# Reordering the first attention layer of a two-layer attention and mixture-of-experts kernel on all engines

## The reference, cut to what matters

```python
xn = ln(x, g_norm)
q = (xn @ Wq).reshape(b, n, 16, 64)            # 16 heads of 64
k, v = split(xn @ Wkv)                         # one shared key/value head
k, v = concat([null_k, k]), concat([null_v, v])
q = l2norm(q) * q_scale                        # l2norm: t / max(norm(t), 1e-12)
k = l2norm(k) * k_scale
sim = q @ k^T * 8 + bias                       # masked, causal
out = softmax(sim) @ v
return ln(out @ Wout, g_out)
...
x = x + ternary_ffn(attention_0(x))            # first layer
x = x + mixture_of_experts(attention_1(x))     # second layer: no l2norm of q and k
```

## Time and profile before

| | |
|---|---|
| three timed runs | 679.77, 673.1, 679.88 us; median 679.77 |
| profiled execution | 673.8 us |
| its span, first to last instruction | 672.1 us |
| granted TensorE clock, mean over the span | 0.921 of full speed |
| busy: PE, DVE, ACT, POOL | 73%, 63%, 56%, 48% of the span |
| first layer's scores | from 55.8 us on, 16 batches |
| second layer's scores | from 348.4 us on, 16 batches |

### The profile page before, as it was taken

How to read it: one execution, slowest core, us unless ns; L and a number is a source line. 1 busy time by engine, 2 the same in 40 slices (tenths; PEclk the granted TensorE clock), 3 DMA queues, 4 the chain that set the end, 5 groups by cost and what they waited for, 6 DMA issues and landing times.

```text
span 672.1 us, 13998 instructions
## 1 busy us (share of the span) xinstructions
PE 493.2 (73%) x3209; PEld 397.8 (59%) x3209; DVE 426.6 (63%) x2098; ACT 378.4 (56%) x1473; POOL 322.8 (48%) x397
## 2 busy tenths in 40 slices
PE   1057788888788887888679899999886505999930
PEld 0034566666566655756668787787775403887820
DVE  2644788778877888446367989888997421344313
ACT  1036876777677767465178787878685101444310
POOL 5235476446654683176343434252347660345660
PEclk9986999999999998999679999999999855999975
DMA  3822075220000000000000000000001112344316
GB/s 102 213 61 74 13 133 109 68 64 9 4 6 6 4 6 4 1 1 1 4 5 9 6 8 5 6 6 5 7 18 44 35 44 50 103 116 124 88 38 193
DMA packets 53757, 30.14 MB, mean 45 GB/s; under 512 B 19994, under 2 KB 50131, under 8 KB 53715
## 3 DMA queue, kind: packets, MB, share of 16 engines
q1 hardware_dynamic: 51154, 24.77, 15.7%
q0 software_dynamic: 2560, 4.90, 2.3%
HBM read 16.13 MB, written 11.42 MB: 41 GB/s over the span
## 4 chain that ended last, share of the span: by engine, by line
PE 39%; DVE 18%; issue 14%; SPq 10%; ACT 7%; DMA 6%; POOL 5%; DVEq 1%; POOLq 0%; ACTq 0%
PE psS L810 5%; PE psS L1061 5%; PE psQ L782 4%; DVE sc L1430 4%; DMA slot_rows<-Y,dest_u 4%; PE psQ L777 3%; PE psQ L1051 3%; PE psO L846 3%; ACT sc L1143 2%; SPq L448 2%; ACT qT L1124 2%; PE psA L865 2%; DVE centred L1494 2%; SPq L431 2%; DVE OT L1451 2%
## 5 line engine op out<-in xcount | busy, mean ns | idle before, releaser
L1143 ACT ACTIVATE sc<-sc,negmax 128x97 f32<-128x97 f32 (+3 forms) x512 | 179.2, 355 | 55.3 <-DVE negmax L1430 55.1
L1430 DVE CUSTOM_DVE_ANT_0 sc<-psS,wide_buf 128x97 f32<-128x97 f32 (+3 forms) x512 | 93.7, 239 | 65.2 <-PE psS L810 64.2
L810 PE MATMUL psS<-kk,qT 128*128 128x194 f32 (+3 forms) x512 | 102.7, 323 | 17.9 <-DVE negmax L1430 17.8
L613 POOL TENSOR_TENSOR wide_buf<-bias,mask 128x132 f32<-128x132 f32 (+3 forms) x128 | 104.3, 841 | 6.1 <-DVE negmax L1430 4.2
L810 PEld LDWEIGHTS psS<-kk,qT 128*128 128x128 f32 x512 | 81.1, 194 | 34.6 <-issue 30.7
L1143 ACT ACTIVATION_READ_ACCUMULATOR sc<-sc,negmax 128x1 f32 x512 | 97.8, 191 | 0.0
L1442 DVE TENSOR_TENSOR pn<-sc,rsum 128x128 f32<-128x128 f32 (+3 forms) x128 | 71.5, 559 | 8.7
L865 PE MATMUL psA<-Wo,OT 128*128 128x128 f32 (+1 forms) x512 | 65.5, 282 | 1.7 <-DVE OT L1451 1.7
L865 PEld LDWEIGHTS psA<-Wo,OT 128*128 128x128 f32 x512 | 62.9, 196 | 3.0 <-DVE OT L1451 2.6
L562 POOL TENSOR_TENSOR qrn<-qssc,half 128x9 f32<-128x9 f32 (+1 forms) x32 | 57.3, 1789 | 2.7
L588 POOL TENSOR_SCALAR qssc<-qss 128x9 f32<-128x9 f32 (+1 forms) x32 | 13.0, 405 | 91.8 <-DVE qss L1416 91.8
(11 more groups left out here) (256 smaller groups left out, 1022.2 us busy)
## 6 DMA issues: line engine op xcount, KB each, us to landing
eW<-in_L_ffn_W SPq DMA_DIRECT2D x16, 256.0 KB, 3.0
slot_rows<-empty SPq DMA_DIRECT2D x2, 1390.0 KB, 11.7
xb<-slot_rows SPq DMA_DIRECT2D x16, 139.0 KB
vp_u<-vp SPq DMA_DIRECT2D x128, 8.0 KB
choice_rows<-zero_row SPq DMA_DIRECT2D x8, 256.0 KB, 3.0
wide_buf<-choice_rows SPq DMA_DIRECT2D x8, 256.0 KB, 4.5
Wq<-in_L_cond_Wq SPq DMA_DIRECT2D x2, 512.0 KB, 6.9
vp_u<-vp SPq DMA_DIRECT2D x64, 16.0 KB
```

What stands on the lines that cost most here:

```text
L613: pool.tensor_tensor(unit_masked(i, u).rearrange("p h e k -> p (h e) k"), unit_bias(layer, u).rearrange("p h e k -> p (h e) k"), mask[laye ...
L810: m = pe.matmul(psS[:, h, 0:2 * w], qT[i][:, h, u].rearrange("p m q -> p (m q)"), kk[i][:, :, 0:w], start=True, stop=True)
L1143: m = act.activation(v, v, ACT.Exp, bias=negmax[:, u, g:g + 1], scale=-1.0, accum_out=psum_row[:, u, g:g + 1])
L1430: dve.tensor_tensor_reduce(sc[u][:, h, e, :], unit_psum(u)[:, h, e, :], unit_masked(i, u)[:, h, e, :], -1.0, -FAR, ALU.add, ALU.min, accum ...
```

## The change

Only the order and the waits of the first attention layer change, and one small operation moves from one engine to another. The arithmetic is the same.

1. The floor of the squared sums goes from POOL (`q_norm`) to DVE (`floored`), one for each half, shortly behind the sum. POOL keeps only the power (`q_rsqrt`).
2. `project_in` of the first layer is split: keys and values (`project_values`), first half of the queries, second half (`project_heads`). It projects `b+1` in the pass of `b`, instead of `b+2` at its end: the first half ahead of the scores of unit 0, the second half between units 0 and 1.
3. `turn_queries` is split. The first half of `b+1` stays in the pass of `b`, the second half opens the pass of `b+1`. On DVE `queries_norm` is split likewise.
4. Unit 3 of a batch is pushed back into the next pass on ACT and DVE: its `biased`, exponentials and `divide`, and `divide` of unit 2.
5. `queries` on ACT counts each half on `q_ready`, so a half of the projection waits only for its own half.
6. In the out norm the mean and variance (`moments`) are taken ahead of `keys_in`, and `out_centred` behind it.
7. On POOL the masks of units 0 to 2 stand between the two powers. `hide` stands at the end of its pass instead of the start.

The second layer's lists keep their order; its functions are only written out by themselves.

```diff
+            def q_rsqrt(b, h):
+                lo, hi = ((0, 9), (9, HEADS + 1))[h]
+                apart(pool, (s["q_floor"], 2 * b + h + 1))
+                rsqrt(qrn[:, lo:hi], qssc[:, lo:hi], hi - lo, s["rn_ready"])
...
+            def attention_first():                       # POOL
+                def batch(b, i):
+                    if not first:
+                        q_rsqrt(b, 1)
+                        values_set(0, b, i)
+                    if not last:
+                        mask_bias(0, b + 1, 0, 1 - i)
+                        mask_bias(0, b + 1, 1, 1 - i)
+                        mask_bias(0, b + 1, 2, 1 - i)
+                        q_rsqrt(b + 1, 0)
+                        mask_bias(0, b + 1, 3, 1 - i)
+                    if isinstance(b, int) and b in (3, NB - 2, NB - 1):
                         hide(b)
...
+            def project_heads(b, h, i):                  # PE
+                held(pe, s["q_ready"], 2 * b + h - 1)
+                pe.matmul(psQ[:, h, :], xnT[i][:], Wq[0][:, 512 * h:512 * (h + 1)],
+                          start=True, stop=True).then_inc(s["q_psum"], 1)
...
+                    turn_queries(b, 1)
+                    if not last:
+                        project_values(b + 1, 1 - i)
+                        project_heads(b + 1, 0, 1 - i)
+                    if not first:
+                        turn_probs(b - 1, 2, 1 - i)
+                    scores(0, b, 0, i)
+                    if not first:
+                        values_pair(b - 1, 1 - i)
+                    if not last:
+                        project_heads(b + 1, 1, 1 - i)
+                    scores(0, b, 1, i)
+                    if not first:
+                        turn_probs(b - 1, 3, 1 - i)
+                    if not first and not no(b, 1):
+                        project(0, b - 2, i, not last)
+                    scores(0, b, 2, i)
+                    if not first:
+                        values(b - 1, 1 - i)
+                    scores(0, b, 3, i)
+                    if not last and not no(b, NB - 2):
+                        turn_input(0, b + 2, i)
+                    if not last:
+                        turn_keys(b + 1, 1 - i)
+                        turn_queries(b + 1, 0)
+                    turn_pair(b, i)
...
+                    queries(0, b, i)                     # ACT
+                        pair_T(b - 1, 1 - i)
+                        squares(b + 1, 0)
+                        weights(4 * (b - 1) + 3, 3)
+                        weights_T(b - 1, 2, 1 - i)
+                    weights(4 * b, 0)
+                        squares(b + 1, 1)
+                        weights_T(b - 1, 3, 1 - i)
+                    weights(4 * b + 1, 1)
+                    weights(4 * b + 2, 2)
+                        input_T(0, b + 2, i)
+                        keys_T(0, b + 1, 1 - i)
...
+            def floored(b, h):                           # DVE
+                lo, hi = (0, 9) if h == 0 else (9, HEADS + 1)
+                apart(dve, (s["ss_step"], 2 * b + h + 1))
+                dve.tensor_scalar(qssc[:, lo:hi], qss[:, lo:hi], 1e-24, None, ALU.max).then_inc(s["q_floor"], 1)
...
+                    queries_norm(b, 1)
+                        divide(b - 1, 2)
+                        outputs(b - 2, 1, i)
+                        biased(n - 1, 3, 1 - i)
+                        input_norm(0, b + 2, i)
+                        sum_squares(b + 1, 0)
+                        values_in(0, b + 1, 1 - i)
+                        floored(b + 1, 0)
+                    biased(n, 0, i)
+                        divide(b - 1, 3)
+                        outputs(b - 1, 0, 1 - i)
+                    biased(n + 1, 1, i)
+                    divide(b, 0)
+                        queries_norm(b + 1, 0)
+                        sum_squares(b + 1, 1)
+                        out_stats(0, b - 2, i)
+                        floored(b + 1, 1)
+                    biased(n + 2, 2, i)
+                        moments(b - 2, i)
+                        keys_in(b + 1, 1 - i)
+                        out_centred(b - 2, i)
+                    divide(b, 1)
```

More of the change, by code:

```diff
@@ L640, in batch, with attention_second @@
+            def attention_second():
+                def batch(b, i):
+                    if not no(b, NB - 1):
+                        for u in range(UNITS):
+                            mask_bias(1, b + 1, u, 1 - i)
+                        values_set(1, b + 1, 1 - i)
+                    if not (no(b, 0) or no(b, 1)):
                         output_rstd(b - 2, i)
-                    if layer == 1 and isinstance(b, int) and b >= NB - 3:
+                    if isinstance(b, int) and b >= NB - 3:
@@ L670, in _ @@
+                for t in range(GROUPS[1][0] + 2, GROUPS[1][1]):
+                    scatter(t, 1)
+            attention_first()
             pool.wait_ge(s["f_c2"], 1)
```

468 lines of the change are left out of this document (231 added, 237 removed).

## The result

The changed kernel takes 655.67 us (median of four executions, 654.18 to 657.25); the kernel before, beside it, 679.83 (673.1 to 680.26). The ratio is 0.967, 95% interval 0.960 to 0.973. The forecast was 655 (643 to 671). The waits that it named are the ones that went, but two terms of its sum, the layer's end and the second layer, were wrong by 4.1 and 4.6 us in opposite directions. The profiled execution took 655.14 us, its span 653.4 instead of 672.1: 18.7 us less. One execution among all of this document, the fourth with the floors back on GpSimd, ran at a mean granted clock of 0.734 where its neighbours had 0.92 to 0.93 and took 712.62 us; what lowered the clock is not known, and its ratio leaves it out.

A forecast was written before the change was run, and what follows sets the result against it. Hand-overs between lists worked through in order were taken to bound the first layer's pass. Passes -19.0, start -1.6, interval +1.1 and end -1.9 sum to -21.4 us: 652.4 or 658.4, middle 655 us, range 643 to 671.

The forecast's parts named there:

- The waits that it named: First layer, VectorE waiting for scores ahead of units 3 and 0: about 1.1 and 1.0 us a pass, both to go.
- The pass: First layer's loop: 13.36 us falls to 12.0, between 11.4 and 13.4; over 14 passes -19.0 us.
- the new one: First layer's pass: VectorE's first sum waits for ScalarE's squares, about 0.15 us.
- Contention: First layer's pass: GpSimd's mask additions hold VectorE's divides, 0.5 us a pass taken, bounds 0 and 1.9.
- The "slower" rival: First layer: GpSimd holds VectorE instructions with two SBUF inputs, from 2.0 us a pass on; three held gives 688 us; 8%.
- Floors: First layer's pass: two more VectorE instructions on 8 or 9 columns, 0.14 us each, +0.29 us.
- SP's six copies of the values ... Nothing: First layer's pass: the copies start with GpSimd's `values_set`, the values are read a whole pass later; no cost.
- The start: Ahead of the first layer's first scores: only half the projection stands there, scores near 54.2, -1.6 us (0 to -2.5).
- The interval: First layer, batch 14 to 15: `hide` ahead of the power that opens batch 15 makes it 1.1 us longer.
- The end: From batch 15's first scores to the first layer's last centred output, 26.55 us: -1.9, bounds +2 and -3.
- Second layer and feed-forward ... only start earlier: Behind the first layer: the lists are the same and only start earlier, no change in their length.
- The level: Whole time: runs before lie at 679.8 or 673.1; the sum gives 658.4 or 652.4, the middle 655 was taken.

The follow-up runs named there:

- the floors' experiments: Changed kernel with the floors back on GpSimd: 651.98 us, ratio 0.963; kernel before with only the floors moved to VectorE: 680.19 us beside 678.79.
- The wait experiment: Changed kernel with one more TensorE wait behind batch 15's scores, for the last exponentials before turning unit 2's probabilities: 664.49 us.
- two variants of the old order: Kernel before with only the floors moved to VectorE: 680.19 us; kernel before with SyncE's table loads behind the values' copies: 673.07 us.

## Why the prediction was right, and where it was not

- **The pass** was predicted at 12.0 and is 11.87. Both removed waits are gone and the new one is 0.2 (0.15 predicted). VectorE's own work bounds the pass, as the floors' experiments show (0.39 us of work and 0.37 of pass; 0.33 and 0.34 in the old order). It is not alone: of the 0.33 us that the held divide gives back only 0.18 reach the pass, and TensorE is busy for 11.33 of its 11.87 us. I had reasoned mostly with the projection and the transposes; what carries most of the gain is the deferral of unit 3 with the divide kept ahead of it (1.2 of 1.61 us). The rest, 0.4 us and the 0.35 that the floors take back, is open: the split of the projection gives nothing, and the split of the queries' transposes, the order of the out norm and that of the masks were not tried by themselves. The prediction worked out VectorE's need, 11.08 us, from a pass of 13.43; with the 13.48 that four passes take it is 11.13, and its 12.0 would have been 0.05 more.
- **Contention** was taken as 0.5 us and is 0.18: one divide is held, by 0.33 us on the mean, and half of that is hidden. The "slower" rival needed 2 us and was far off. The Trainium skill ("GPSIMD Engine Reference", Key points) names the shared SBUF interface and VectorE instructions "with two SBUF inputs"; for the divide of 384 columns beside masks the trace agrees (894 for 563 ns), for the key's product under a power it does not (336 ns, against 0.35 us in the earlier trace rows). Counting masks alone was right here. The prediction laid two divides under masks: unit 2's is held, in every other pass, and unit 0's takes 292 ns as before.
- **Floors**, +0.29 a pass, are +0.34 to +0.37: 0.16 to 0.17 us each rather than 0.14, which is 0.33 us of instructions.
- **"SP's six copies of the values ... Nothing"** is a step that failed. It holds in the steady pass and not in the one from batch 1 to 2, where SP has 32 loads to issue first: 15.65 us, of which 4.3 go when the loads are moved. The term came from reading one pass in the middle and multiplying by 14. Over the 14 passes the sum had 19.0 us and 16.3 was measured: a steady pass in place of the reckoned one gave 1.9 more, this one and the first took back 5.0, the others gave 0.4.
- **The start** gave 2.0 for 1.6. That close a figure is in part luck, since the clock's level alone moves the first scores by 1.4 us (52.45 and 53.83 us with the same lists). **The interval** from 14 to 15 gave +1.0 for +1.1; its wait of 0.75 us for the power behind `hide` is in the trace, and moving `hide` takes it away.
- **The end** gave 6.0 for 1.9. I had counted instructions at the durations of the old trace, those were partly at the low clock, and the wait of 2.13 us ahead of them does not appear in the prediction. The wait experiment shows that 3.9 us hang on TensorE's idle time there, the wait and the clock behind it together.
- **"Second layer and feed-forward ... only start earlier"** was wrong by 4.6 us: 1.3 between the layers (from the last centred output to the second layer's first scores it is 56.94 us for 55.68), 5.6 in the interval with the stall, less 2.3 that the rest of the second layer and what follows it are shorter (0.5 up to that interval, 1.8 behind it), for which no run shows a cause. The 5.6 can't be charged to the change: two variants of the old order have the stall too, and the profile of before happens to be without it. The stall is gone in both kernels whose scatters were moved; whether the scatters cause it, and by what means they could stop VectorE or TensorE, stays open.
- **The level.** Against the profiled execution the sum gave 652.4 and 655.14 was measured. Taking the middle of the two levels of before gave 655, and the median is 655.67: that it is so close is luck, an error of 2.7 in the sum and a choice of level worth 2.6 the other way, and within the sum two errors of over 4 us that nearly cancel.

## What to carry to other kernels

Once the waits in a loop are gone, look at what the busiest in-order engine itself has to do. Here two floors of 0.16 us on VectorE cost their whole time, and it paid to leave them on the engine that idles, even at the price of a longer way. When an instruction must wait, look at what stands behind it on its engine before pricing the wait; the divide behind a waiting bias was 0.8 of 1.2 us here. Read the first passes apart from the steady one: a queue that is free later may still be working off its preloads. And before a longer interval elsewhere is charged to the change, look for it in variants of the old kernel.

## What was not expected of the hardware

- An idle time can cost TensorE more than its length: 2.13 us (before) and 2.67 us (experiment) were followed by projections of 3.35 and 3.25 us, against 1.95 to 2.05 without such a wait; in the experiment 5.4 us in all. It need not: 2.23 us at 268.30 of the changed kernel left the clock at 1.00.
- GpSimd's additions of masks (two SBUF inputs) hold a VectorE divide of 384 columns by 0.62 to 0.68 us when the mask started first (1.18 to 1.24 for 0.56 us); when the divide started first, by 0.05 us, the mask was held instead (1.26 for 0.89). GpSimd's powers do not hold a product of 128 columns (336 ns).
- VectorE or TensorE stood still for 2.4 to 5.3 us, with no releaser on the core, beside or shortly behind GpSimd's scatters in ten of twelve kernels, and not in the two in which those were moved.
